# Seeding the bank of a product with minus the mean, instead of adding the mean's product afterwards

## The reference, cut to what matters

```python
t1 = einsum('nchw,he->ncew', x, p1)            # x here is _gn(x)
t3 = conv(t1, p3)                              # depthwise 9x9
t4 = conv(t3, p4)                              # grouped 5x1
t5 = einsum('ncew,ewf->ncf', t4, p5[:, :, 0, :])
t6 = conv(t5[:, :, None, :], p6)[:, :, 0, :]   # depthwise over f, three taps
out = einsum('ncf,nfp->ncp', t6, t2.reshape(n, 3 * c, h * w)) / sqrt(3 * c)
x = x + out
```

## Time and profile before

| | us |
|---|---|
| median of 3 runs | 375.95 (375.14 to 376.3) |
| the profiled execution: time | 376.2 |
| the profiled execution: span on the core | 374.4 |
| one step of the loop, from 204.63 to 262.75 us (6 steps) | 9.69 |

### The profile page before, as it was taken

One profiled execution on the slowest core, in us unless ns is written; L12 is line 12 of the kernel. 1 busy time (PEld: TensorE's weight loads), 2 busy tenths in 40 slices (PEclk: granted clock), 3 DMA queues, 4 the chain that ended last, 5 costly groups with the idle time before them and its releaser, 6 DMA issues.

```text
span 374.4 us, 5177 instructions
## 1 busy us (share of the span) xinstructions
PE 298.2 (80%) x1679; PEld 247.9 (66%) x1679; DVE 324.7 (87%) x585; ACT 243.9 (65%) x384; POOL 255.1 (68%) x245
## 2 busy tenths in 40 slices
PE   0698756999999999349899999999999999884000
PEld 0254421999998996148688888888888888652000
DVE  1799987999998984995977999999999999779793
ACT  2389996576667678963566666666666666430791
POOL 9835464799998796097667888888888888742000
PEclk9999995899999999866999999999999999897555
DMA  8999930000243136871400000000000000000399
GB/s 171 167 200 199 208 74 1 3 0 2 55 110 78 35 86 180 299 312 35 191 1 3 0 2 0 2 2 0 2 1 2 0 3 0 0 2 0 128 403 365
DMA packets 18622, 31.07 MB, mean 83 GB/s; under 512 B 4292, under 2 KB 12228, under 8 KB 18596
## 3 DMA queue, kind: packets, MB, share of 16 engines
q1 hardware_dynamic: 18404, 30.32, 29.5%
q0 software_dynamic: 192, 0.42, 0.4%
HBM read 17.89 MB, written 8.39 MB: 70 GB/s over the span
## 4 chain that ended last, share of the span: by engine, by line
DVE 46%; PE 21%; ACT 16%; issue 7%; POOL 4%; DMA 2%; SPq 2%; DVEq 0%; POOLq 0%; ACTq 0%
PE wide L758 6%; DVE st L1007 5%; DVE x_sb L1000 4%; DVE x_sb L1112 4%; ACT d_split L585 4%; DVE y_sb L1046 4%; ACT t_hi L498 3%; DVE s_lo L909 3%; DVE sty L1052 3%; PE wide L231 2%; DVE y_sb L1039 2%; PE wide L233 2%; ACT t_f L504 2%; PE wide L232 2%; ACT toe L509 2%
## 5 line engine op out<-in xcount | busy, mean ns | idle before, releaser
L418 POOL TENSOR_TENSOR s_f<-toe,ci_mask 128x640 f32<-128x640 f32 x32 | 40.7, 1271 | 13.4 <-DVE s_lo L911 13.4
L474 POOL TENSOR_TENSOR g_lo<-y_sb,g_hi 128x1024 fp32r<-128x1024 f32 x15 | 36.2, 2410 | 15.2 <-ACT y_sb L635 15.2
L634 ACT ACTIVATE g_hi<-x_sb,rs 128x1024 fp32r<-128x1024 f32 x16 | 21.5, 1342 | 35.6 <-POOL rs L459 32.3
L891 DVE STREAM_TRANSPOSE xa<-x_ring 128x1024 f32<-128x1024 f32 x16 | 32.7, 2060 | 8.5 <-DMA x_ring<-in_x 8.1
L909 DVE TENSOR_TENSOR s_lo<-s_f,s_hi 128x640 fp32r<-128x640 f32 x32 | 35.6, 1111 | 4.6 <-ACT s_hi L524 4.5
L231 PE MATMUL wide<-g_hi,t_hi 128*128 128x512 f32 x96 | 38.2, 397 | 0.1
L233 PE MATMUL wide<-g_hi,t_lo 128*128 128x512 f32 x96 | 37.8, 394 | 0.0
L232 PE MATMUL wide<-g_lo,t_hi 128*128 128x512 f32 x96 | 37.7, 393 | 0.0
L450 POOL TENSOR_TENSOR g_lo<-y_sb,g_hi 128x1024 fp32r<-128x1024 f32 x15 | 36.0, 2399 | 0.8 <-ACT g_hi L608 0.8
L523 ACT CAST s_hi<-s_f 128x640 fp32r<-128x640 f32 x32 | 23.3, 729 | 11.8 <-POOL s_f L421 11.6
L421 POOL TENSOR_TENSOR s_f<-toe,v_mask 128x128 f32<-128x128 f32 x32 | 28.0, 874 | 0.0
(11 more groups left out here) (176 smaller groups left out, 1006.6 us busy)
## 6 DMA issues: line engine op xcount, KB each, us to landing
x_ring<-in_x SPq DMA_DIRECT2D x32, 256.0 KB, 6.4
x_sb<-in_x SPq DMA_DIRECT2D x8, 1024.0 KB, 7.1
out<-x_sb SPq DMA_DIRECT2D x7, 1024.0 KB, 5.0
d_sb<-t_out SPq DMA_DIRECT2D x58, 68.0 KB, 2.1
out<-x_sb SPq DMA_DIRECT2D x2, 512.0 KB, 2.6
p_raw<-in_p SPq DMA_DIRECT2D x8, 96.0 KB, 10.0
d_sb<-t_out POOLq DMA_DIRECT2D x6, 68.0 KB, 3.3
w_raw<-in_conv_w SPq DMA_DIRECT2D x1, 256.0 KB, 7.0
```

Source lines behind the costliest of these rows:

```text
L418: pool.tensor_tensor(s3_f[:, g % 2], toe3[:, g].unsqueeze(2).broadcast_to([128, SHIFTS, CI, E]), ci_mask[:, :].unsqueeze(1).unsqueeze(3).b ...
L474: pool.tensor_tensor(g2_lo[:, :], y_sb[:, n, :], g2_hi[:, :].bitcast(F32), ALU.subtract).then_inc(s["g2_lo"], 1)
L891: dve.transpose(xa[:, n % 2], x_ring[:, n // 2 % XR, n % 2, :].rearrange("p (h w) -> p w h", w=W)).then_inc(s["xa"], 1)
```

## The change

For k >= 3 the bank of t5 is first written by ScalarE with minus the mean of image k times t5 of ones (`seed(k)`), and the twelve matmuls of `t5_product(k)` all accumulate onto it. The bank then holds t5(x) - mean * t5(ones), so the three taps give the finished u, and `u_mean(k)` goes for k = 3 to 16. Minus t5 of ones is copied once, in step 0, from its bank to SBUF (`minus_ones`). `u_mean` stays for k = 1 and 2. The semaphore that frees the bank is now waited for by ScalarE, and TensorE waits for the seed.

```diff
         p5_rest = [put("p5_rest_hi", [JC, NF], F32R), put("p5_rest_lo", [JC, NF], F32R)]
+        minus_ones = put("minus_ones", [NF])
...
         @block.scalar
         def _(act):
+            link = chained(act, "act")
...
+            def seed(k):
+
+                act.wait_ge(s["u"], k)
+                act.activation(t5_bank(k)[:, 0:NF], minus_ones[:, :], ACT.Identity,
+                               scale=gs1[:, k - 1, 0:1]).then_inc(s["seed"], 1)
+
...
                 if t >= 2:
                     z_evacuate(t - 2)
+                if t >= 1 and t + 3 <= N:
+                    seed(t + 3)
                 if 1 <= t <= N:
                     g2_full_and_high(t - 1)
                 if t == 0:
                     act.wait_ge(s["d_lo"], 6)
                     act.wait_ge(s["d_lo_pool"], 2)
                     act.copy(p5_rest[0][:, :, :], p5_sb[:, :, :]).then_inc(s["p5_rest_hi"], 1)
+                    link(act.mul(minus_ones[:, :], t5_bank(0)[:, 0:NF], -1.0))
+                    seed(3)
                 if t + 1 < N:
                     g1_full(t + 1)
...
             def t5_product(k):
 
                 if k >= 3:
-                    pe.wait_ge(s["u"], k)
+                    pe.wait_ge(s["seed"], k - 2)
...
                     mm = split_product(t5_bank(k)[:, 0:NF], (d_split[:, n, 0, jc, :], d_split[:, n, 1, jc, :]),
-                                       (p5_parts[0][:, jc, :], p5_parts[1][:, jc, :]), jc == 0, jc == JC - 1)
+                                       (p5_parts[0][:, jc, :], p5_parts[1][:, jc, :]), k < 3 and jc == 0, jc == JC - 1, k >= 3)
...
+            def u_parts(k):
+
+                return max(1, 2 * k) if k < 3 else k + 3
+
             def u_next(k):
                 dst, _, tap = u_views(k)
-                dve.wait_ge(s["u_part"], max(1, 2 * k))
+                dve.wait_ge(s["u_part"], u_parts(k))
...
-                ins.then_inc(s["u_part"] if k else s["u"], 1)
+                ins.then_inc(s["u"] if k == 0 or k >= 3 else s["u_part"], 1)
...
-                if u <= N:
+                if u == 2:
                     u_mean(u)
```

More of the change, by code:

```diff
@@ L203, in build @@
                  "sel_mm sel_ev p5_pm w_f w_hi w_lo s_f s_hi s_lo conv t3_hi t3_lo t4_mm t4_ev "
-                 "st1 gst_mm gst gst_q rs1 t5 u_act u t6_mm t6_hi t6_lo g1_f g1_hi g1_lo o_half o_mm x1 "
+                 "st1 gst_mm gst gst_q rs1 t5 u_act u seed t6_mm t6_hi t6_lo g1_f g1_hi g1_lo o_half o_mm x1 "
                  "st2 st2_mm st2_v st2_e st2_r g2_hi g2_f g2_lo z_mm z_ev zh y_mm y_rd y sty "
-                 "fin_s fin_q fin relu res dve pool stored").split()
+                 "fin_s fin_q fin relu res dve pool act stored").split()
         s = {n: sem("s_" + n) for n in names}
@@ L227, in rows_of, with split_product @@
             return v.rearrange("p (r b j) -> p r b j", j=J, b=2)
[L229 to L233, removed]
+        def split_product(ps, w, m, start, stop, seeded=False):
+            nc.tensor.matmul(ps, w[0], m[0], start=start, stop=False, skip_group_check=seeded)
+            nc.tensor.matmul(ps, w[0], m[1], start=False, stop=False, skip_group_check=seeded)
+            return nc.tensor.matmul(ps, w[1], m[0], start=False, stop=stop, skip_group_check=seeded)
         def t5_bank(k):
```

## The result

The change makes the kernel slower: 379.34 us median of 5 runs (378.37 to 380.2) against 375.14 us of the kernel before in the same runs (374.15 to 376.3), a ratio of 1.012 with a 95% interval of 1.0088 to 1.0152. The forecast was 379.6 us, with 377.3 to 382.3 as its range. The profiled execution took 379.2 us, 3.0 more than the one of before.

What follows compares the result with a forecast made beforehand. TensorE's own 9.67 us step was taken as the bound, level with VectorE. From the profiled 376.2 us, -0.6 (end) + 2.2 (ScalarE wait) + 1.9 (start) = +3.5 gave 379.7, 379.45 against the median, stated as 379.6; range 377.3 to 382.3.

Steps and rivals of the forecast that it cites:

- What bounds the kernel: Middle steps: TensorE's own step is 9.67 us, level with VectorE's 9.69, so relieving VectorE gives 0.02 us a step.
- The wait on ScalarE: Loop: the seed waits for VectorE's `u_next`, the activation behind it starts 1.11 us later, steps take 9.92 us: +2.2 us.
- The long loop: Two steps, group average through POOL's L450 and the next `out_product` to the next group average: 19.82 us, 9.91 a step.
- The start: Step 0: the first seed waits for the stalled `u_mean(2)`, delaying ScalarE, POOL and the second `out_product`: +1.9 us.
- The end: Last step that had `u_mean`: the group average no longer waits 0.65 us for VectorE: -0.6 us.
- Faster: Rival: VectorE really sets the step, each step gives back up to 0.617 us, down to 367.6 us; chance 0.07.
- The covered loop: Rival: ScalarE's delay stays under the smaller spare of 0.8 us, so the loop loses nothing: 377.5 us; chance 0.10.
- The clock at the start: Rival: TensorE's clock falls after standing about 2.1 us before the second `out_product`, costing 1.4 to 1.7: 381.1 us; chance 0.16.
- The collision: Rival: each step POOL's L458 takes the SBUF port before VectorE's L1046, +2 us over ten steps: 381.7 to 382; chance 0.14.

Runs made afterwards that it cites:

- no_mean: The kernel before with `u_mean` left out for images 3 to 16 and nothing in its place: 373.13 us, ratio 0.9963.
- the late start: The change with seeds from k = 4 between g2_full_and_high's two activations and the first seed behind `g1_high(1)` in step 1: 373.65 us, ratio 0.9972.
- wait_for_next: The kernel before with only a wait for `u_next` of the same step added on ScalarE, ahead of g2_full_and_high: 374.76 us, ratio 1.0018.
- seed_between: The change with the seeds from k = 4 between the two activations of g2_full_and_high, first seed unmoved: 376.34 us, ratio 1.0044.
- next_first: The change with VectorE's `u_next` placed ahead of `y_own`: 383.4 us, ratio 1.0239.
- spare_activation: The change with one more 128x384 activation, to a spare tile, right behind each seed from k = 4: 385.26 us, ratio 1.0287.

## Why the prediction was right

**What bounds the kernel.** Shown. TensorE's step was read as 9.67 us from one early step in which VectorE was idle; no_mean gives 9.65 with VectorE relieved everywhere. The relief was priced at 0.02 us a step and is 0.04.

**The wait on ScalarE.** Shown, and to the size: 1.11 us forecast for L642 against the group average, 1.09 measured (4.22 - 3.13); 9.92 us a step forecast, 9.93 measured. The long loop is the one that binds, as L846 does not wait for L475. Over the loop it is 109.25 - 106.58 = 2.7 us where I had 2.2: I counted ten steps of 0.23 less some slack, but steps 3 to 13 are eleven, and the first of them bears it already (9.90 us). VectorE's waits of 0.8 us a step ahead of `norm_factors` are there too: 0.41 on average at L1034 and 0.42 at L1043, just before it.

**The start.** The wait behind the stalled `u_mean(2)` cost 10.58 - 8.63 = 1.95 us in the profiles without a fall of the clock, 1.9 forecast. That the first seed's place makes it is shown by the late start, 8.50.

**The end.** -0.6 forecast. The two profiles differ by 2.17, but 1.6 of it need not come with `u_mean`: wait_for_next has `u_mean` and much the same two stops (0.93 and 0.67 us), its clock stays at 1.00, and its end is 18.23. So the 19.85 of the kernel before holds a fall of the clock that not every execution with these stops has. From 18.23 to 17.66, the end of no_mean, it is 0.57.

**The sum.** 1.95 + 2.67 - 0.57 = 4.05 us against 3.5 forecast; the medians are 4.2 apart. How much of the clock's falls the medians hold on either side is not known; single executions of the kernel before lie between 371.36 and 377.54 us. The forecast missed by more than the 0.26 us between 379.6 and 379.34 suggest: it was counted from a median of 375.95, which is 375.14 in the runs with the change, so +3.65 was forecast where +4.20 was measured, and that the two misses nearly cancel is luck. The difference of the two profiles, 3.1 us in span, is smaller than the 4.05 by chance of the clock and of the part ahead of the loop: the change's has 1.56 us of it at the start, that of before 1.6 at the end, and the first group average comes 1.0 us earlier in the change's.

**The rivals.** Faster, 367.6, is refuted by no_mean: with VectorE relieved the step stays at 9.65. The covered loop is what wait_for_next and seed_between show for the wait alone and for the work alone, but not for both together. The clock at the start had a chance of 0.16; it came in one profile of four. The collision did not come: L451 did end where L1062 was due, POOL's L459 was issued 0.07 us ahead of it, and L1062 took its usual 1.29; it was POOL's L460, right behind, that was held, 0.82 us where it took 0.27 at 188.35 with no L1062 beside it. By the rule of the Trainium skill (SBUF — State Buffer, Who interferes with whom) the first to issue should have kept the pair; with a one-element instruction nothing of the kind shows. With the long ones it does: L483 and L1008 here, L468 and L1062 in next_first. So such collisions have a price, 0.67 us in a step of next_first, but with another instruction of POOL than the one that the rival named.

## What to carry to other kernels

Before relieving the engine that holds the chain, look for a stretch in which it was idle: the length of a step there is the floor that the next engine sets. A wait that is moved to an engine with idle time is not free if something urgent is queued behind it; take the spare of each consumer behind the wait, and put the new instruction where its semaphore is already set. And when an instruction is moved, ask what the instruction that it changes places with will stand beside.

## What the runs showed of the hardware

- TensorE's clock fell in single executions and at different places: in the profile of before after stops of 0.94 and 0.65 us (19.85 us for the last two intervals), in the change's after 2.06 us (12.14 us), in next_first's after 1.92. Much the same stops left it at 1.00 elsewhere: 0.93 and 0.67 us in wait_for_next (18.23 us), 2.06 to 2.07 in seed_between, next_first and spare_activation (10.58 to 10.60 us). 0.4% of a profile's time (1.6 of 375 us) can be this alone, so two profiles are to be compared interval by interval.
- ScalarE's activation of 384 columns took 586 ns from SBUF to PSUM, and 601 ns from the same SBUF tile to SBUF. spare_activation has both one behind the other, 186 to 365 us:

```profile
L606 ACT ACTIVATE spare<-minus_ones,gs 128x384 f32<-128x384 f32 x13 | 7.8, 601 | 0.0
L603 ACT ACTIVATE bank<-minus_ones,gs 128x384 f32<-128x384 f32 x13 | 7.6, 586 | 34.2 <-DVE u_sb L1003 34.2
```

  The Trainium skill (ScalarE: Activation LUTs, Step-by-step: what each stage is for) calls a write to PSUM the faster one; the trace agrees, and it is 15 ns. From PSUM to SBUF (L597 of the change) it took 586 ns as well.
- Twelve matmuls that accumulate onto a bank written by ScalarE take TensorE no longer than twelve of which the first overwrites: a step of 9.67 us in seed_between, 9.65 to 9.69 in kernels without seeds.
